# Layer 0 gives the tokens transposed in one step, and down works on transposed sums

## The reference

```python
x = x + einsum('bct,bcd->bdt', x, w0[ia]) + bias0[ia][:, :, None]   # layer 0: 64x64 per sample
# layer 1: gated MLP, each of gate, up and down with a low-rank adapter of rank 16 chosen per sample
lin(v, W, A, B) = v @ W + (v @ A[ia]) @ B[ia]
x = x + lin(silu(lin(x, Wg, Ag, Bg)) * lin(x, Wu, Au, Bu), Wd, Ad, Bd)   # 512 -> 2048 -> 512
x = x + x @ W2.T + scale[ib] * ((x @ A2[ib].T) @ B2[ib].T)          # layer 2: 512 -> 512
x = x + einsum('bct,bcd->bdt', x, w3[ic])                           # layer 3: 64x64 per sample
```

## Time and profile before

| | before |
|---|---|
| median of three runs | 766.19 us |
| profiled execution | 767.69 us, span 765.9 |
| TensorE matmuls busy | 727.8 us (95%) |
| VectorE busy | 601.1 us (78%) |
| ScalarE busy | 284.8 us (37%) |
| GpSimd busy | 255.3 us (33%) |
| products L1376 | 1344 matmuls |
| down L1474 | 768 matmuls |
| mean granted clock | 0.99 |

### The profile page before, as it was taken

One profiled execution on the slowest core, in us unless ns is written; L12 is line 12 of the kernel. 1 busy time (PEld: TensorE's weight loads), 2 busy tenths in 40 slices (PEclk: granted clock), 3 DMA queues, 4 the chain that ended last, 5 costly groups with the idle time before them and its releaser, 6 DMA issues.

```text
span 765.9 us, 10652 instructions
## 1 busy us (share of the span) xinstructions
PE 727.8 (95%) x3626; PEld 606.9 (79%) x3626; DVE 601.1 (78%) x1010; ACT 284.8 (37%) x508; POOL 255.3 (33%) x489
## 2 busy tenths in 40 slices
PE   6779889999999999989899999999999999899997
PEld 4547678888888888878778888888888888788886
DVE  7975768797878778799898979787888877766675
ACT  3445523333424333434353334242434333134232
POOL 4724231515223232350327162534425231241100
PEclk9979999999999999999999999999999999999999
DMA  7366520313212121203723232221212061212112
GB/s 209 87 81 194 164 80 29 104 37 108 83 56 83 55 84 56 83 27 111 248 59 109 71 103 73 70 86 58 89 55 85 28 192 32 79 29 70 42 55 83
DMA packets 65941, 66.02 MB, mean 86 GB/s; under 512 B 31712, under 2 KB 48096, under 8 KB 65888
## 3 DMA queue, kind: packets, MB, share of 16 engines
q1 hardware_dynamic: 57248, 45.92, 19.9%
q0 software_dynamic: 7296, 19.41, 8.7%
q10 hardware_dynamic: 1344, 0.02, 0.1%
HBM read 56.94 MB, written 8.39 MB: 85 GB/s over the span
## 4 chain that ended last, share of the span: by engine, by line
PE 84%; DVE 10%; issue 2%; ACT 2%; DMA 1%; POOLq 0%; POOL 0%; ACTq 0%; DVEq 0%
PE bank L1376 36%; PE bank L1474 22%; PE bank L1384 7%; PE bank L1633 6%; PE bank L1483 4%; PE bank L1622 2%; PE bank L1326 1%; PE bank L1599 1%; PE bank L1639 1%; DVE XC L882 1%; PE bank L1650 1%; PE bank L1611 1%; DVE hid L1001 1%; PE bank L1353 1%; DVE hs L1007 1%
## 5 line engine op out<-in xcount | busy, mean ns | idle before, releaser
L1376 PE MATMUL bank<-XC,WC 128*128 128x512 f32 x1344 | 332.9, 394 | 6.7 <-DVE tmp L975 2.2
L1376 PEld LDWEIGHTS bank<-XC,WC 128*128 128x128 f32 x1344 | 245.5, 190 | 54.8 <-issue 4.7
L1474 PE MATMUL bank<-wds,hs 128*128 128x512 f32 x768 | 187.6, 394 | 6.6 <-DVE X L1017 3.3
L1474 PEld LDWEIGHTS bank<-wds,hs 128*128 128x128 f32 x768 | 142.9, 190 | 35.8 <-DVE wds L960 3.8
L398 POOL DMA_INDIRECT BR<-in_L_cond_Bu_dram,boffs x64 | 71.9, 1124 | 265.7 <-DVE BL L954 251.1
L398 POOL DMA_INDIRECT BR<-in_L_cond_Bg_dram,boffs x64 | 76.1, 1189 | 95.2 <-DVE BL L954 80.2
L620 ACT ACTIVATE hs<-hid 128x512 fp32r<-128x512 f32 x64 | 40.3, 630 | 164.4 <-DVE hid L1001 111.4
L1017 DVE TENSOR_TENSOR X<-bank,X 128x512 f32<-128x512 f32 x128 | 86.5, 686 | 17.5 <-PE bank L1474 15.3
L614 ACT ACTIVATE hid<-hid 128x512 f32<-128x512 f32 x48 | 30.4, 633 | 148.4 <-DVE hid L984 75.9
L1384 PEld LDWEIGHTS bank<-UT,BL 128*128 128x128 f32 x512 | 76.4, 190 | 10.0 <-issue 2.1
L1384 PE MATMUL bank<-UT,BL 128*128 128x256 f32 x512 | 81.9, 283 | 1.3 <-ACT hid L611 1.3
(11 more groups left out here) (152 smaller groups left out, 827.9 us busy)
## 6 DMA issues: line engine op xcount, KB each, us to landing
RW<-in_L_cond_Wg_dram SPq DMA_DIRECT2D x16, 512.0 KB, 4.4
RW<-in_L_cond_Wu_dram SPq DMA_DIRECT2D x16, 512.0 KB, 5.1
RD<-in_L_cond_Wd_dram SPq DMA_DIRECT2D x16, 512.0 KB, 3.5
out_dram<-XR SPq DMA_DIRECT2D x16, 256.0 KB, 2.0
X<-in_x_dram SPq DMA_DIRECT2D x8, 256.0 KB, 6.2
udp<-in_x_dram SPq DMA_DIRECT2D x8, 256.0 KB, 4.5
x1park<-RD SPq DMA_DIRECT2D x8, 256.0 KB, 4.2
x2park<-X SPq DMA_DIRECT2D x8, 256.0 KB, 2.5
```

Of the source, the lines that this page charges most:

```text
L1376: last = nc.tensor.matmul(psum[:, :], WC[:, t, left, a, k, :], XC[:, right, b, k, :], start=(first and k == 0 and n == 0), stop=(k == 1 an ...
L1474: last = nc.tensor.matmul(psD[j % 2][:, :], hs[:, f, a, j * P:(j + 1) * P], wds[:, f, b, :], start=(f == 0 and n == 0), stop=(f == 1 and n ...
```

## The change

Layer 0 takes x as weights (with a step of four floats) and the w0 block as the moving side, so that four f32 matmuls give x1 already transposed; the identity is added when GpSimd places the block, and a fifth matmul, ones of 40 rows against a table `bsel` of the bias (high and low part), adds the bias. x1_sum, x1_bias, transposes and add_identity are gone. `xr_copy` writes to XA (first half) or XB (second), through four psum banks. Six pairs of the second half come before the third product of unit 0, two behind it; x is loaded four pairs ahead. The sums T1 to T4 of the first half lie in hid, since XA stays as the running sum. `down` takes wds as weights, with a step of four floats, and hs as the moving side; `evict` adds to XA, and both parks are in that layout. In the tail lora_down is turned too, transposes2 is gone, identities are added to W2 (`w2_identity`) and w3 (`w3_identity`), x3_sum and y_sum are gone, and `y_out` on ScalarE copies the output. The orders on all engines are changed accordingly; `x3_high` and `x3_low` read psD, and load_d(0) waits for the last layer 0 only. VectorE's tail loop becomes x2_sum (both), xt_low, x3_low (both), u2_mask, w3_low (both).

```diff
+        XIN = 4
+        xin = [udp[:, s * FEAT:(s + 1) * FEAT] for s in range(2)] + [RD[:, s, :] for s in range(2)]
+        bsel = wds[:, :, :, :].rearrange("p f a o -> p (f a o)")[0:BROWS, :]
+        bias_high = BL[32:BROWS, 0, 0, 0:POS]
+        xfirst = XB[:, :, :].rearrange("p k t -> p (k t)").rearrange("p (a t) -> p a t", t=FEAT)
...
+        xc_raw[0].update({T3: hid[:, 0:2, :], T1: hid[:, 0:2, :], T2: hid[:, 2:4, :], T4: hid[:, 2:4, :]})
...
+        def by_feature(v):
+            return v.rearrange("p (o k) -> p k o", k=KT)
...
-                load_xin(HP)
-                load_xin(HP + 1)
+                for p in range(HP, HP + XIN):
+                    load_xin(p)
                 load_idx(2, idx_c)
                 load_u(0)
                 load_g(1)
+                load_xin(HP + 4)
+                load_xin(HP + 5)
                 for n in range(ADAPTERS):
                     sp.dma_start(ad_raw[:, :, n * RANK:(n + 1) * RANK],
                                  ad[n].rearrange("(k p) r -> p k r", p=P)).then_inc(s_ald, 16)
+                    if n == 1:
+                        load_xin(HP + 6)
+                    if n == 3:
+                        load_xin(HP + 7)
+                load_d(0)
                 for p in range(HP, PAIRS):
-                    if p + 2 < PAIRS:
-                        load_xin(p + 2)
                     park_x1(p)
-                    if p == HP + 3:
-                        load_u(1)
-                load_d(0)
+                load_u(1)
...
-                        last = nc.gpsimd.tensor_copy(w0bd_of(p)[rows, rows].rearrange("p (c f) -> p c f", f=KT),
-                                                     w0tab[rows, bass.ds(cols[half], RANK), :])
+                        last = nc.gpsimd.tensor_tensor(w0bd_of(p)[rows, rows].rearrange("p (c f) -> p c f", f=KT),
+                                                       w0tab[rows, bass.ds(cols[half], RANK), :],
+                                                       ident[rows, rows].rearrange("p (c f) -> p c f", f=KT), ALU.add)
...
-                pool.wait_ge(s_boffs, 1)
-                gather_b(0)
                 for g in range(2, 4):
                     late = adapters(8 * g, 8)
                     for p in range(4 * g, 4 * g + 4):
                         place_w0(p, late[2 * (p - 4 * g):2 * (p - 4 * g) + 2])
+                pool.wait_ge(s_boffs, 1)
                 pool.wait_ge(s_w0c, PAIRS)
+                gather_b(0)
                 gather_b(1)
...
+                u_high(0, 0)
+                xr_copy(HP)
+                xr_copy(HP + 1)
                 xc_high(0, T2)
-                u_high(0, 0)
+                u_high(0, 1)
+                xr_copy(HP + 2)
+                xr_copy(HP + 3)
                 xc_high(0, T1)
-                u_high(0, 1)
+                xr_copy(HP + 4)
                 xc_high(0, T4)
                 b_high(0, 0)
+                xr_copy(HP + 5)
+                xr_copy(HP + 6)
+                xr_copy(HP + 7)
...
+                def y_out(d, q):
+                    act.wait_ge(c_l3, 2 * d + q + 1)
+                    if d >= 2:
+                        act.wait_ge(c_out[d % 2][q], 16 * (d // 2))
+                    nc.scalar.activation(y[d % 2][q], psR[q][:, :], ACT.Copy).then_inc(c_y, 1)
...
+                    x3_high(d, 0)
+                    x3_high(d, 1)
                     if d + 3 < DUOS:
                         bd_high(d + 3)
                     if d + 1 < DUOS:
                         u2_high(d + 1)
-                    x3_high(d)
+                    if d >= 1:
+                        y_out(d - 1, 0)
+                        y_out(d - 1, 1)
+                    w3_high(d, 0)
+                    w3_high(d, 1)
+                y_out(DUOS - 1, 0)
+                y_out(DUOS - 1, 1)
...
+                def w2_identity():
+                    dve.wait_ge(s_w2ld, 16)
+                    for k in range(KT):
+                        own_block = w2_raw[:, k, k * P:(k + 1) * P]
+                        last = nc.vector.tensor_tensor(own_block, own_block, ident[:, :], ALU.add)
+                    last.then_inc(s_w2i, 1)
...
+                    sums = XA[:, j % KT, j // KT * 512:(j // KT + 1) * 512]
+                    nc.vector.tensor_tensor(sums, psD[j % 2][:, :], sums, ALU.add).then_inc(s_evict, 1)
...
+                    if unit == ALL - 2:
+                        w3_identity(0)
+                        w3_identity(1)
+                    if unit == ALL - 1:
+                        w2_identity()
...
+                bias_table()
+                biases(0)
                 gather_rows()
-                biases()
+                g_combine(0)
+                biases(1)
+                nc.vector.memset(w0second[:, :, :], 0.0).then_inc(s_zero, 1)
+                layer3_zeros()
                 move_matrices()
                 masks()
-                x1_sum(0)
-                x1_sum(1)
-                x1_sum(2)
-                g_combine(0)
-                x1_sum(3)
                 raw_low(G, 0)
-                x1_sum(4)
-                add_identity()
-                x1_sum(5)
-                x1_sum(6)
-                x1_sum(7)
                 xc_low(0, B11)
+                xc_low(0, B21)
+                sums_low(G, 0)
...
+                x2_sum(0, 0)
+                x2_sum(0, 1)
                 table_low(2)
                 table_low(3)
-                x2_sum(0, 0)
-                x2_sum(0, 1)
                 evict(unit, 4)
                 evict(unit, 5)
+                xt_low(0)
                 table_low(4)
                 table_low(5)
-                xt_low(0)
                 evict(unit, 6)
                 evict(unit, 7)
-                x2_sum(1, 0)
-                x2_sum(1, 1)
+                u2_mask(0)
...
                 def layer0(p):
                     pe.wait_ge(s_w0c, p + 1)
                     if p < HP:
                         pe.wait_ge(s_xload[p], 16)
                     else:
-                        pe.wait_ge(s_xin[p % 2], 16 * ((p - HP) // 2 + 1))
-                    if p >= HP + 2:
-                        pe.wait_ge(s_x1b, p - HP - 1)
-                    elif p >= 2:
-                        pe.wait_ge(s_x1, p - 1)
-                    nc.tensor.matmul(psD[p % 2][:, :], w0bd_of(p), x_of(p), start=True, stop=True).then_inc(s_l0, 1)
-                def transposes(p):
-                    if p < HP:
-                        pe.wait_ge(s_x1, p + 1)
-                    else:
-                        pe.wait_ge(s_x1b, p - HP + 1)
-                    if p >= 2:
-                        pe.wait_ge(s_xr, p - 1)
+                        pe.wait_ge(s_xin[p % XIN], 16 * ((p - HP) // XIN + 1))
+                    if p >= 4:
+                        pe.wait_ge(s_xr, p - 3)
                     for k in range(KT):
-                        last = nc.tensor.transpose(psR[p % 2][:, k * P:(k + 1) * P],
-                                                   x1_of(p).rearrange("t (c k) -> t k c", k=KT)[:, k, :], ident[:, :])
-                    last.then_inc(s_tr, 1)
+                        nc.tensor.matmul(l0_bank(p)[:, k * P:(k + 1) * P], by_feature(x_of(p))[:, k, :], w0bd_of(p),
+                                         start=(k == 0), stop=False, skip_group_check=True)
+                    if p % HP == 0:
+                        pe.wait_ge(s_bias, p // HP + 1)
+                    nc.tensor.matmul(l0_bank(p)[:, :].rearrange("p (k t) -> p k t", k=KT), ones[0:BROWS, :],
+                                     bsel[:, p * P:(p + 1) * P].unsqueeze(1).to_broadcast([BROWS, KT, P]),
+                                     start=False, stop=True, skip_group_check=True).then_inc(s_l0, 1)
...
                         select(h, 1)
+                        layer0(HP + 4)
                     select(h, 2)
                     select(h, 3)
+                    if h == 0:
+                        layer0(HP + 5)
...
-                            last = nc.tensor.matmul(psD[j % 2][:, :], hs[:, f, a, j * P:(j + 1) * P], wds[:, f, b, :],
+                            last = nc.tensor.matmul(psD[j % 2][:, :], by_feature(wds[:, f, a, :])[:, j % KT, :],
+                                                    hs[:, f, b, j // KT * 512:(j // KT + 1) * 512],
...
+                    if unit == 0:
+                        layer0(HP + 6)
+                        layer0(HP + 7)
                     c11_product(n, G, 2 * unit)
...
+                layer0(HP)
+                layer0(HP + 1)
                 adapters_in(0, 1)
+                layer0(HP + 2)
+                layer0(HP + 3)
...
+                def lora_down(d):
                     h = d // (DUOS // 2)
-                    if q == 0:
-                        pe.wait_ge(s_bdl, d + 1)
-                        pe.wait_ge(s_udl, h + 1)
+                    pe.wait_ge(s_bdl, d + 1)
+                    pe.wait_ge(s_udl, h + 1)
                     if d == 0:
```

(31 more changed lines are left out.)

440 lines of the change are left out of this document (171 added, 269 removed).

## The result

Beside four runs of the kernel before (median 766.39 us, 766.14 to 767.77) the changed kernel takes 789.77 us (788.48 to 790.66, 4 runs). The ratio is 1.030, 95% interval 1.0281 to 1.0319: slower by 3%. The forecast was 745.0 with a range of 738 to 755, and it put 0.91 on faster. It was wrong in sign and by 44.8 us. The profiled execution took 789.54 us, its span 787.7.

A forecast was written before the change was run, and what follows sets the result against it. TensorE (84% of the chain) was taken as the bound where it runs without gaps, VectorE's list at the start; 12.1 (start) + 1.3 (unit 1) + 7.8 (tail) = 21.2 us less than 766.19 gave 745.0, range 738 to 755.

The forecast's parts named there:

- A load's duration is not its spacing: Down's stepped weight loads: 0.118 us spacing hides behind 0.227, so cost zero; upper end 23.8 us over 768 products.
- lora_down (priced at 0.06 a duo, upper end 13.4): Tail: 12 matmuls of 256 columns take 1.42 us for 1.36; with load length exposed, 13.4 us more.
- rival E: Slower: down's stepped loads are exposed; at 31 ns a load 769 us, with lora_down 782; chance 0.08.
- Layer 0 at 1.17 us a pair: Start: eight pieces at 0.118 plus a 512-column bias matmul at 0.227; two pairs on the path, 2.4 us.
- Clock: Start: a gap of some 4 us before the third product brings a low clock, 1.7 us lost.
- The start: GpSimd late, at 41.5: First adapter rows land at 41.5 after GpSimd's block placing and gathers; third product starts at 44.0, not 39.6.
- rival B: Start: GpSimd is the gate, adds at 1.14 each, 6 to 9 us more, 751 to 754; chance 0.17.
- Unit 1: Wd loaded over 30 us sooner removes a 1.28 us ScalarE stall: 1.3 us less; first product at 71.1.
- The tail: Removing 64 transposes of x2 and reordering makes a duo 11.0 us for 11.7; tail 7.8 us less.
- 3.9 + 4.4 - 0.3 = 8.0: Tail: 3.9 us earlier at duo 0's layer 2, 4.4 over six duos, 0.3 waiting for duo 0's successor.
- Rival D: Tail does not hold: VectorE's queue late at tables or in each duo, half the gain goes, 749; chance 0.07.

The follow-up runs named there:

- the gather and the order together: Changed kernel with features in 128-blocks, 128-row bias product, first gather earlier, four pairs later, ScalarE's high halves and first rank move ahead: 750.90 us, ratio 0.9806, the study's best.
- the run with 128 rows: Changed kernel, weights still stepped, with the bias product of layer 0 over 128 rows instead of 40: 776.42 us, ratio 1.0127.
- the order alone: ScalarE's high halves and first rank move put earlier, in the changed kernel with features in 128-blocks: 762.52 us with a 40-row bias product, 757.57 with 128 rows.
- the blocks kernels: Changed kernel with all features in blocks of 128, so no weight load is stepped: 761.74 us with the 40-row bias product, 756.90 with 128 rows.
- the earlier gather: Changed kernel with features in 128-blocks and 128-row bias product; first gather after half the second half's blocks, pairs 12 to 15 later: 753.24 us, ratio 0.9831.
- the kernel with the warm-up of 512 columns: Changed kernel with features in 128-blocks and 40-row bias product; 20 warm-up products of 512 columns for 24 of 128: 758.61 us, ratio 0.9889.
- 44 warm-up products of 128 columns: Changed kernel with features in 128-blocks and 40-row bias product; 44 warm-up products of 128 columns in place of 24: 761.9 us, ratio 0.9946.
- the four blocks kernels with 128 rows: Changed kernel, features in 128-blocks, 128-row bias product: plain 756.90 us, ScalarE and rank-move order changed 757.57, first gather earlier 753.24, both 750.90.

## Why the prediction was wrong, point by point

Taken in the order of the experiments, the 44.8 us between 789.77 and 745.0 are 28.0 for stepped loads, 4.8 for the 40 rows, 6.0 for the gather and the order together, and 5.9 that remain. The order of counting matters: alone, in the changed kernel, the 40 rows are worth 13.4, so the first two costs overlap in the start.

**"A load's duration is not its spacing" (the middle, and lora_down).** This is the step that failed, and it carries most of the miss. It took the spacing of 0.118 us from stepped loads of transposes and applied it to those of ordinary products. Those loads last 311 to 328 ns instead of 208, and packed ones 190; lora_down's spacing became 0.233 us for 0.118, down's 0.235 to 0.244 for 0.227. The costs are 9.5 us in down (priced at 0, its upper end 23.8), 10.1 in lora_down (priced at 0.06 a duo, upper end 13.4) and 8.6 in layer 0, for which no upper end was given at all: 28.2 of 44.8. It is rival E's mechanism, at 0.4 of E's price in down and 0.75 in lora_down, with layer 0 as a place that E did not name. The sentence itself was true, since even a load of 311 ns added only 8 to 17 ns to a product's spacing; the row it was drawn from was of another kind of load. And that row was not read to the end: the prediction says that the trace does not show the step in the spacing, while its own figures are 0.118 us for stepped transposes and 0.10 for packed ones.

**Layer 0 at 1.17 us a pair.** The size is right for packed pieces and 128 rows at the high clock (1.13). The changed kernel had 2.37 to 2.89. The term for a matmul of 40 rows was taken from matmuls of 128, and nothing in the trace of before bounded it. With the stepped pieces beside it that cost 13.4 us by the run with 128 rows, with packed ones 4.8. The eight pairs of the first half were not charged at all, since VectorE's list was taken as the bound there; at 2.89 us a pair TensorE came first.

**Clock.** The forecast charged the low clock for 1.7 us. By the spacing the changed kernel stayed at the lower level up to about 38 us.

**The start: GpSimd late, at 41.5.** The gathers of the changed kernel were issued from 33.61, landing within 3.3 to 4.6 us, near the forecast, but the rows were split at 59.03 only: on ScalarE their split stood behind the copies of pairs 8 to 12, and those behind TensorE. The prediction listed what VectorE waits for and not what ScalarE queues. That this order costs time here is not shown: TensorE had only 0.64 us of idle time ahead of the third product (61.72), so its own slow pairs came first, and the order alone gained nothing in the blocks kernels. VectorE's waits of that kind were 4.34 and 4.87 us:

```profile
46.68 1.23 DVE L904 TENSOR_TENSOR XC<-hid,XC 128x1024 fp32r<-128x1024 f32 x1 [4.34 <-ACT XC L542]
...
54.51 1.22 DVE L904 TENSOR_TENSOR XC<-hid,XC 128x1024 fp32r<-128x1024 f32 x1 [4.87 <-ACT XC L542]
```

Once the pairs are quick, GpSimd is the gate after all, rival B: the gain of the earlier gather bears it out, at 3.7 or 6.7 us for the 6 to 9 that B had. B put it on the adds (0.51 forecast, 10.62 / 16 = 0.66 measured); as much of it is the copies ahead of them, 10.38 us.

**Unit 1.** A gain of 1.3 was forecast for the earlier Wd. Instead there is a stall of 2.54 us for VectorE's sum at L1002, in the changed kernel and in every variant of it. The kernel before had 1.03 for the same sum, beside the 1.28 for ScalarE; the sum's rows before and after:

```profile
93.79 1.65 PE L1376 MATMUL bank<-XC,WC 128*128 128x512 f32 x6 [1.03 <-DVE tmp L975]
```

```profile
103.01 2.48 PE L1372 MATMUL bank<-XC,WC 128*128 128x512 f32 x6 [2.54 <-DVE tmp L1002]
```

VectorE runs without a pause ahead of it: the stall by ScalarE went, and the length of VectorE's queue took its place. In the best kernel the first product of unit 1 starts at 73.92, 2.8 us behind the forecast; with the 1.3 that is 4.1 of the 5.1 us by which its span (749.8) exceeds 744.7.

**The tail.** Right, once the loads are packed: from the down at 616.98 to layer 2 of duo 7 it is 134.45 us before and 126.27 in the blocks kernel (618.23 to 744.50), 8.2 less; forecast 3.9 + 4.4 - 0.3 = 8.0. The duo is 11.06 for 11.0, and the wait ahead of duo 0's successor is 0.27 for 0.3. From duo 7's layer 2 to the end of the span it is 14.9 for 14.6. Rival D does not occur. The chance put on E (0.08) was low for a cost whose upper end had been worked out at over 37 us.

## What to carry to other kernels

Read what a weight load costs from a load of the same kind with the same step; where TensorE has no gaps, what a load adds to the spacing of its product counts in full (12 ns in the mean made 9.5 us over 768 products), and that is neither nothing nor the load's excess over the product. A layout that removes an operation can be had with packed blocks instead of steps. Before moving work onto an engine, write down the queue of the engine that empties its results as well. When a stage of TensorE comes out at twice its price, look at the spacing of like matmuls first, since the level of the clock shows there even where the trace holds no change of it.

## What the runs showed of the hardware that was not expected

- A weight load of 128 x 128 in f32 or fp32r took 190 ns packed, 195 with a step of two floats and 311 to 328 with four, all at the upper level of the clock. At the lower level a packed one had 333 (the first eight pairs of the blocks kernel). Transposes with a step of four had 208 against 140.
- A product of 512 columns with 40 of 128 rows took 0.43 us where one with 128 rows takes 0.31 in the same place (high clock), and the eight f32 pieces beside it 0.99 against 0.81. With it between the pairs TensorE, busy without a gap, was granted 0.50 of its clock from about 11 to about 35 us (the kernel with the warm-up of 512 columns); with 128 rows the rise came at about 12.8 by the spacing. Why is open: nothing here separates the rows from the slower pace that they bring.
- 44 warm-up products of 128 columns, back to back for 9.5 us, stayed at the lower pace; 20 of 512 columns left it within 6.3 us.
- GpSimd's 16 copies of 128 x 128 took 4.50 us in the changed kernel and 10.36 to 10.43 in the four blocks kernels with 128 rows. The layout is not the reason, as they took 5.47 in the blocks kernel with 40 rows, nor are blocks needed, as they took 7.62 in the changed kernel with 128. In the changed kernel VectorE was mostly waiting (4.27 busy of 10 us), in the blocks kernel with 128 rows it was not (8.25 of 10). The two stretches:

```profile
20.00:30.00 10.00, 10.00 (x34) 7.80 (x33) 4.27 (x5) 5.28 (x8) 9.01 (x23) 1.00 0.23 70
```

```profile
20.00:30.00 10.00, 6.94 (x40) 6.00 (x38) 8.25 (x9) 5.53 (x10) 9.68 (x16) 0.84 0.23 82
```

The Trainium skill (SBUF — State Buffer, section Who interferes with whom) has a VectorE instruction with two SBUF inputs shut out a GpSimd instruction that reads SBUF; the copies agree with it, their median going from 288 to 618 ns over the kernel. No run changed VectorE alone, so the cause is not shown. Slower copies put GpSimd's gather later, which fits that the 11.4 us gained at the first product by the 128 rows (blocks) were 6.8 at the third, 5.9 at unit 1's first product and 4.8 at the end.
